# Two layer norms whose last scaling moves from VectorE to ScalarE

## The reference

```python
def _layernorm(x, axis=-1, eps=1e-05):
    m = jnp.mean(x, axis=axis, keepdims=True)
    v = jnp.var(x, axis=axis, keepdims=True)
    return (x - m) / jnp.sqrt(v + eps)
...
        fc_sc = values @ W + b
        d = jnp.sum(adjacency, axis=1)
        d_inv_sqrt = 1.0 / (jnp.sqrt(d) + OVERFLOW_MARGIN)
        laplacian = adjacency * d_inv_sqrt[:, None] * d_inv_sqrt[None, :]
        return laplacian @ fc_sc
...
        adj_hat = adj + jnp.eye(adj.shape[0], dtype=adj.dtype)
        d_inv_sqrt = 1.0 / jnp.sqrt(jnp.sum(adj_hat, axis=1))
        adj_norm = adj_hat * d_inv_sqrt[:, None] * d_inv_sqrt[None, :]
        out = adj_norm @ (X @ W) + b
        return jax.nn.relu(out)
...
    x = _layernorm(x + _L0_gnn_ref(x, adj, L0_gnn_W, L0_gnn_b), axis=-1)
    x = _layernorm(x + _L1_gnn_ref(x, adj, L1_gnn_W, L1_gnn_b), axis=-1)
```

## Time and profile before

| | before |
|---|---|
| median of 3 runs | 1884.22 us (1883.65 to 1885.18) |
| profiled execution | 1884.51 us |
| its span, first to last instruction | 1882.3 us |
| mean granted clock of PE | 0.964 of full speed |
| PE busy | 1655.4 us, 88% |
| DVE busy | 1264.2 us, 67% |
| ACT busy | 739.5 us, 39% |

### The profile page before, as it was taken

How to read it: one execution, slowest core, us unless ns; L and a number is a source line. 1 busy time by engine, 2 the same in 40 slices (tenths; PEclk the granted TensorE clock), 3 DMA queues, 4 the chain that set the end, 5 groups by cost and what they waited for, 6 DMA issues and landing times.

```text
span 1882.3 us, 17109 instructions
## 1 busy us (share of the span) xinstructions
PE 1655.4 (88%) x6136; PEld 1117.6 (59%) x6136; DVE 1264.2 (67%) x1854; ACT 739.5 (39%) x889; POOL 66.2 (4%) x127
## 2 busy tenths in 40 slices
PE   0257889999999999968999999999999999999996
PEld 0123344444444444456777777787787787777775
DVE  1444556776876567277655656545547899999996
ACT  5553342111000000045444444444446666666663
POOL 0000000000000000000000000000000000000000
PEclk9778899999999999989999999999999999999998
DMA  9999999998877976155666665656567999999991
GB/s 387 421 421 421 421 422 393 416 404 343 366 312 290 367 298 232 28 213 212 250 232 227 229 227 209 213 219 228 196 216 313 421 397 363 353 356 361 362 367 78
DMA packets 85906, 573.38 MB, mean 305 GB/s; under 512 B 10400, under 2 KB 10656, under 8 KB 20288
## 3 DMA queue, kind: packets, MB, share of 16 engines
q1 hardware_dynamic: 76320, 541.23, 72.6%
q0 software_dynamic: 9504, 31.07, 4.7%
HBM read 556.79 MB, written 15.47 MB: 304 GB/s over the span
## 4 chain that ended last, share of the span: by engine, by line
PE 67%; DVE 18%; DMA 11%; issue 3%; ACT 1%; SPq 0%; DVEq 0%; POOL 0%; ACTq 0%
PE acc L659 28%; PE acc L683 12%; PE acc L685 12%; PE acc L684 12%; DVE low L806 7%; DMA lent<-adj_tiles 6%; DMA own<-adj_tiles 2%; DVE stats L781 1%; DMA own<-adj_far 1%; DMA lent<-adj_far 1%; DVE run L817 1%; DVE o L795 1%; PE turned L595 1%; DVE z L930 1%; DVE h L884 1%
## 5 line engine op out<-in xcount | busy, mean ns | idle before, releaser
L683 PE MATMUL acc<-high,feat_high 128*128 128x512 f32 x1336 | 536.1, 401 | 70.6 <-DVE low L806 59.5
L659 PE MATMUL acc<-lent,feat 128*128 128x512 f32 x1168 | 522.8, 607 | 20.9 <-DVE feat L856 13.5
L685 PE MATMUL acc<-high,feat_low 128*128 128x512 f32 x1336 | 526.7, 394 | 0.0
L684 PE MATMUL acc<-low,feat_high 128*128 128x512 f32 x1336 | 525.9, 394 | 0.0
L806 DVE TENSOR_TENSOR low<-own,high 128x1024 fp32r<-128x1024 f32 x330 | 390.5, 1220 | 177.7 <-ACT high L702 175.1
L702 ACT CAST high<-own 128x1024 fp32r<-128x1024 f32 x330 | 338.2, 1052 | 197.1 <-PE acc L685 190.4
L659 PEld LDWEIGHTS acc<-lent,feat 128*128 128x128 f32 x1168 | 226.2, 195 | 304.5 <-issue 288.6
L817 DVE TENSOR_TENSOR run<-run,lent 128x2048 f32<-128x2048 f32 x135 | 309.3, 2291 | 135.8 <-DMA lent<-adj_tiles 129.7
L683 PEld LDWEIGHTS acc<-high,feat_high 128*128 128x128 f32 x1336 | 254.1, 190 | 139.2 <-issue 81.5
L685 PEld LDWEIGHTS acc<-high,feat_low 128*128 128x128 f32 x1336 | 254.0, 190 | 55.2
L684 PEld LDWEIGHTS acc<-low,feat_high 128*128 128x128 f32 x1336 | 254.5, 191 | 50.1
(11 more groups left out here) (77 smaller groups left out, 649.3 us busy)
## 6 DMA issues: line engine op xcount, KB each, us to landing
lent<-adj_tiles SPq DMA_DIRECT2D x237, 1024.0 KB, 11.1
own<-adj_tiles SPq DMA_DIRECT2D x197, 1024.0 KB, 5.6
lent<-adj_far SPq DMA_DIRECT2D x60, 1024.0 KB, 23.0
own<-adj_far SPq DMA_DIRECT2D x18, 1024.0 KB, 23.0
x_in<-x_rows POOLq DMA_DIRECT2D x32, 256.0 KB, 4.4
sums_rows<-stage POOLq DMA_DIRECT2D x27, 256.0 KB, 6.4
sums_in<-sums_rows POOLq DMA_DIRECT2D x27, 256.0 KB, 6.3
x_t<-x_cols SPq DMA_DIRECT2D x16, 256.0 KB, 15.6
```

Source lines behind the costliest of these rows:

```text
L659: mm = nc.tensor.matmul(bank, feat0[:, j * Q + q, :], raw(n)[:, q * T:(q + 1) * T], start=(u == plan.first[g] and q == 0), stop=(u == plan ...
L683: nc.tensor.matmul(bank, f_high, a_high[:, chunk], start=(u == plan.first[g] and q == 0), stop=False)
L684: nc.tensor.matmul(bank, f_high, a_low[:, chunk], start=False, stop=False)
L685: mm = nc.tensor.matmul(bank, f_low, a_high[:, chunk], start=False, stop=(u == plan.last[g] and q == Q - 1))
```

## The change

In `Plan` the norm of each row is split. DVE keeps the small steps under the names `scale_x1` and `scale_out`, and ACT gets the scalings as `make_x1` and `make_out`, with the key of ACT's list at the same position. DVE makes `shift` = -mean x `rstd` in one 128x4 instruction, which takes the place of its four scalings. ACT computes `rstd` x `h` + `shift` in four activations of 128 x 128 (function Identity, scale and bias as pointers to one number for each partition). A semaphore `rstd_ready` leads from DVE to ACT. The waits for the turned and stored `x1` and for the stored output move to ACT with the scalings. The core of the diff:

```diff
-            dve.append((lo_key(split, 5), "make_x1", i))
+            dve.append((lo_key(split, 5), "scale_x1", i))
+            act.append((hi_key(split, 5), "make_x1", i))
...
-            dve.append((lo_key(k + 1, 5), "make_out", i))
+            dve.append((lo_key(k + 1, 5), "scale_out", i))
+            act.append((hi_key(k + 1, 5), "make_out", i))
...
+                elif kind == "make_x1":
+                    act.wait_ge(rstd_ready, norm[("scale_x1", i)] + 1)
+                    if i < NB - 1:
+                        act.wait_ge(turn1_done, up(i))
+                        act.wait_ge(x1_stored, 16 * up(i))
+                    for q in range(Q):
+                        ins = nc.scalar.activation(x1[:, q, :], h[:, q, :], ACT.Identity, bias=shift[:, q:q + 1],
+                                                   scale=rstd[:, q:q + 1])
+                    ins.then_inc(x1_ready, 1)
+                elif kind == "make_out":
+                    m = third[i]
+                    act.wait_ge(rstd_ready, norm[("scale_out", i)] + 1)
...
-                for q in range(Q):
-                    ins = nc.vector.tensor_scalar(dst[:, q, :], h[:, q, :], moments[:, q, 0:1], rstd[:, q:q + 1],
-                                                  ALU.subtract, ALU.mult)
-                ins.then_inc(done, 1)
+                nc.vector.scalar_tensor_tensor(out=shift[:, :], in0=moments[:, :, 0], scalar=-1.0, in1=rstd[:, :],
+                                               op0=ALU.mult, op1=ALU.mult).then_inc(rstd_ready, 1)
```

More of the change, by code:

```diff
@@ L399, in gnn_kernel @@
         rstd = put("rstd", [P, Q])
+        shift = put("shift", [P, Q])
         def raw(n):
@@ L455, in gnn_kernel @@
         sdev_ready = sem("sdev_ready")
+        rstd_ready = sem("rstd_ready")
         x1_ready = sem("x1_ready")
@@ L468, in gnn_kernel @@
         dve_step = sem("dve_step")
-        norm = plan.nth(plan.dve, ("make_x1", "make_out"))
+        norm = plan.nth(plan.dve, ("scale_x1", "scale_out"))
         stage_at = plan.nth([e for e in plan.act if e[0] == "empty_right1" or
@@ L742, in _ @@
                 elif kind in ("root_x1", "root_out"):
-                    act.wait_ge(var_ready, norm[(kind.replace("root", "make"), i)] + 1)
+                    act.wait_ge(var_ready, norm[(kind.replace("root", "scale"), i)] + 1)
                     nc.scalar.activation(sdev[:, :], var[:, :], ACT.Sqrt).then_inc(sdev_ready, 1)
+                elif kind == "make_x1":
[10 more added lines that the diff above has]
+                    act.wait_ge(rstd_ready, norm[("scale_out", i)] + 1)
+                    if m >= 2:
+                        act.wait_ge(out_stored[m % 2], 16 * (m // 2))
+                    else:
+                        for r in range(2):
+                            act.wait_ge(sums_stored[r], 16 * len([k for k in stage_at.values() if k % 2 == r]))
+                    for q in range(Q):
+                        ins = nc.scalar.activation(o[:, m % 2, q, :], h[:, q, :], ACT.Identity, bias=shift[:, q:q + 1],
+                                                   scale=rstd[:, q:q + 1])
+                    ins.then_inc(out_ready, 1)
                 elif kind == "x1_columns":
@@ L786, in moments_of_h, with row_scale @@
                 nc.vector.tensor_scalar(var[:, :], moments[:, :, 1], 1e-5, None, ALU.add).then_inc(var_ready, 1)
-            def normalise(m, dst, done):
+            def row_scale(m):
                 dve.wait_ge(sdev_ready, m + 1)
@@ L889, in _ @@
                     moments_of_h()
[L891 to L895, removed]
+                elif kind == "scale_x1":
+                    row_scale(norm[(kind, i)])
                 elif kind == "features1_low":
@@ L939, in _ @@
                     moments_of_h()
[L941 to L948, removed]
+                elif kind == "scale_out":
+                    row_scale(norm[(kind, i)])
 def kernel(x, adj, L0_gnn_W, L0_gnn_b, L1_gnn_W, L1_gnn_b):
```

## The result

The changed kernel takes 1965.59 us (median of 4 runs, 1964.61 to 1973.79), 1.044 times the kernel before, with a 95% interval of 1.0416 to 1.0464. The profiled execution took 1964.61 us with a span of 1962.5. The forecast was 1965 us, from 1930 to 1978.

What follows compares the result with a forecast made beforehand. PE set the pace, with DVE also near its limit in the third sweep, and waited behind DVE's scaling at most norms. 1884.5 + 54.5 for ACT's queue + 26 for PE's clock = 1965 us, range 1930 to 1978.

Steps and rivals of the forecast that it cites:

- The path at each norm: At each norm: last small step, scaling, DVE's next low, PE; now that low also awaits ACT's scalings and a new high.
- 27 regular norms: Rows 11 to 0 of the second sweep and the third's first 15: 1.72 us each, 46.4 us, all reaching PE.
- Partly absorbed: Rival: DVE makes good some of the delay before PE needs it; with half gone about 1911 us; chance 0.09.
- DVE's relief: Rival: with one spare tile of ACT's highs, DVE is 0.87 us earlier at 20 norms; −18 us, 1867; chance 0.04.
- The size at a norm: Last small step to next low: 0.21 + 0.20 + 1.48 + 1.08 = 2.97 us against 1.25, so 1.72 later.
- Row 14: Second sweep: the same delay stands ahead of `x_t`, costing 1.7 us.
- Row 13: Second sweep: ACT's 128x512 cast of features (0.5 us) also stands ahead of the next high; 2.2 us.
- Row 12: Second sweep: `x_t` and `feat_high` stand behind ACT's scalings, `feat_high` still 1.82 us behind `x_t`; PE 3.5 us later.
- The last norm: Tail, where `o` is stored when complete: scaling takes 1.8 us on ACT against 1.11 on DVE, costing 0.7 us.
- The clock: PE's clock falls behind longer stalls: 16 full slow stretches at 1.6 us, 26 us, with 0 and 34 as ends.
- the shares it was made from: Behind 800 us, clock fell after four of four 3.1–4.3 us stalls, one of three 2.4–2.6, three of ten 1.8.
- the rival of the tables: Rival: the new function shares no table set with the square root; 64 loads, 82 us, to 2040; chance 0.01.

Runs made afterwards that it cites:

- one_tile_later: Changed kernel with ACT's scalings put behind the two highs of the next tile (rows 15 to 12 of the second sweep unchanged): 1873.95 us, 0.9937 of the kernel before.
- pe_filled: Changed kernel with ten unused 128x512 matmuls more on PE at the long stall of 25 norms: 1943.49 us, 1.0312 of the kernel before.

## Why the prediction was right, point by point

**The path at each norm.** The step from the order of instructions (no lead of highs) to a wait of DVE behind each shift holds at every one of the 27 regular norms, whose delays differ by 0.02 us, and all of it reached PE: next to nothing of it comes back between them. "Partly absorbed" and "DVE's relief" did not happen. The rival on the other side named its point of decision as one tile of lead, and one_tile_later is that kernel: with the lead the sign turns. It gave 11.4 us on its medians where the rival's price was 18, as rows 14 to 12 still cost 8.7.

**The size at a norm.** 1.72 forecast, 1.78 measured. Its four terms, from the timeline after: 0.21 and 0.20 as forecast, the scalings 1.56 (1782.23 to 1783.79) where 1.48 was taken, and 1.05 from high to low in place of 1.08. Of the scalings the pointer was priced right by rows of other shapes (0.08 to 0.11 against 0.092). The 27 norms gave 48.1 in place of 46.4 us.

**The special rows.** Row 14: 1.79, forecast 1.7. Row 13: 2.29, forecast 2.2. Row 12: 4.4 at the norm, forecast 3.5; 1.1 us of it comes back before the next norm. Row 15: nothing, as forecast. The last norm: its scalings end and the store starts 0.7 us later behind the last small step, as forecast. The timeline of row 12, next to the earlier trace rows, its first line of the kernel before and the others of the changed one:

```profile
836.19 1.16 PE L626 MATMUL mixed<-w_sb,x_t 128*128 128x128 f32 x8 [0.88 <-ACT x_t L747]
...
846.28 0.56 ACT L772 COPY x_t<-mixed 128x512 f32<-128x512 f32 x1
...
846.90 1.85 PE L630 MATMUL mixed<-w_sb,x_t 128*128 128x128 f32 x8 [4.92 <-ACT x_t L772]
...
848.79 1.15 ACT L776 ACTIVATE feat_high<-mixed,scale 128x128 fp32r<-128x128 f32 x4 [1.94 <-PE mixed L630]
```

`feat_high` follows 2.51 us behind `x_t`, where 1.82 was carried over from before: behind a stall of 4.92 us PE makes the weights' products at the lower clock (1.85 us for eight that took 1.16). That is the missing 0.7 us.

**The clock.** 26 us forecast as 16 full slow stretches, 23.0 measured at 14 intervals. The size was right, and pe_filled shows the cause. What the clock did after stalls bears out the shares it was made from: behind 870 us it fell after all nine stalls of 3.3 us and more, after four of the seven of 2.8 us, and after both of 2.5. At eight norms it had fallen already behind the first stall, and the slow tile ate into the second stall and cost nothing:

```profile
1125.10 0.47 PE L687 MATMUL acc<-high,feat_high 128*128 128x512 f32 x1 [2.09 <-DVE low L829]
```

PE waits 2.09 us here in place of 3.3. These eight stalls were 1.7 to 2.1 us, and only behind two of them did the clock fall again. That is one reason why not every norm paid the second price.

**How much of it was luck.** The total came out within 1 us of the forecast because two errors cancel: the norms cost 57.3 us with the last one, forecast 54.5, and the clock 23.0, forecast 26. The number for the clock is partly luck in itself: how many stretches cost something depends on where each falls, and one of the four runs took 1973.79 us. Why that run was 8 us slower than the other three stays open.

**Signs that were off.** PE's waits rose to 101 us (105 forecast) and ACT's wait was 3.4 us (3.2). DVE's waits for highs rose by 91 us, not 70: in the second sweep DVE waits a second time at a norm, as ACT is late with the tile after next too (0.29 us at 1126.38), and it waits longer in the first rows. None of this is on PE's path. The clock fell to 0.95 and 0.94, not 0.96, since slow stretches that cost nothing count in it as well.

**Sums that don't come out.** The upper end of the range, by its own terms (1884.5 + 54.5, 27 × 0.12 and 26 + 8 of clock), is 1976 and not 1978, and the rival of the tables, 82 us on top of the forecast, is 2047 and not 2040. Neither bears on the outcome. The changed kernel loads tables twice in all, for 1.28 us each, at 1.29 and 50.83 us, as the order of instructions said.

## What to carry to other kernels

Before work is moved to an engine because that engine is idle much of the time, read what stands behind it in that engine's own queue, and who waits for that. An in-order engine that runs ahead of its consumer is idle by share, but its lead is what hides the consumer's detours, and one wait at the wrong place takes the whole lead away. If the work must wait for the consumer, put it behind the items that the consumer needs next: here two casts made the difference between 4.4% slower and 0.6% faster. And price a longer stall of PE twice, once for its length and once for the clock behind it.

## What the runs showed of the hardware

- A slow stretch of PE's clock costs something or nothing, by where it falls. At eight of the 14 intervals that grew it cost 1.4 to 1.7 us. Followed by another stall on the same path it is swallowed: behind 860 us and without the one at the very end, pe_filled still has ten such stretches and loses 2.1 us between the norms, the kernel before has five, the changed kernel has 23 and loses 23.0 us at those 14.
- Ten matmuls whose results nobody reads, put into a stall, made the changed kernel 22 us faster (ten at each of 25 norms): the engine's idle time was dearer than useless work.
- An ACTIVATE of 128 x 128 took 483 ns with two pointer operands and 391 with one, both reading SBUF; with one and reading PSUM 368.
